# A vision tower's last mixture-of-experts layer: its outputs combined in groups of four tokens, shared by three engines

## The chip, the cores and the metric

The kernel runs on one core of a Trainium2 chip. The metric is the device time of one execution in microseconds. Three executions of the kernel before are given, with their median, and one more was recorded by the hardware profiler; all durations below are from that one.

## What is computed

The reference is a small vision tower in float32: patches of 128 images become 16 tokens each of 192 features, then follow a quantized attention, a mixture of 4 experts with one choice for each token, a linear attention, and a mixture of 8 experts with two choices. All of them add to the residual h. The change touches the last step alone, and in it only the last sum:

```python
h = h + _L1_ffn_ref(_layernorm(h, axis=-1), ...)
    # _L1_ffn_ref:
    top_p, top_i = jax.lax.top_k(router_probs, 2)
    top_p = top_p / jnp.sum(top_p, axis=-1, keepdims=True)
    ...                                     # the two chosen experts' outputs: o
    o = jnp.einsum('btck,btk->btc', o, top_p)   # p0 * out0 + p1 * out1
```

So each token's new value is h + p0 * (output of its first expert) + p1 * (output of its second).

## The kernel before, in words

Each engine has its own instruction stream, and they meet at semaphores. The residual h lies in SBUF as 128 partitions (images) x 16 tokens x 192 features.

Both mixture layers work alike. VectorE chooses the experts and works out where each token goes (route); SyncE writes the normalized rows to memory (rows_out, four stores of four tokens, lines 305 to 311); GpSimd gathers 128 rows at a time by an indirect DMA and scatters the results of each tile of 128 rows back by another (exchange, lines 403 to 424); TensorE multiplies, ScalarE applies Gelu (gelus), VectorE copies the results out of PSUM (copies). Layer 1 has 39 such tiles. The scattered results lie in DRAM in the tensor made, the first choices of all tokens ahead of the second choices.

When all scatters of the layer have landed, SyncE reads made back in outputs_in (line 326): for the first choice four loads of four tokens each, then four for the second, 384 KB each, into got[0] (the buffer xn) and got[1] (in the arena). Each load has a semaphore of its own. After layer 0 VectorE adds got[0] to h in four steps and goes on; there is only one choice there.

After layer 1 comes the end of the kernel. VectorE runs 32 scalar_tensor_tensor operations on line 1574, each h[:, t] = got[s][:, t] * pk[:, s, t] + h[:, t] for one token t of every image, over 192 elements in each partition: first all 16 tokens of the first choice, a link (the engine waits until its own last result is written), then all 16 of the second. pk holds the two weights of each token. A memset signals h_final, SyncE stores the whole of h in one transfer of 1536 KB (line 353) and waits for it. ScalarE has nothing to do after its last Gelu, and GpSimd nothing after its last scatter.

In the early weights stage (lines 380 to 398) GpSimd adds and multiplies weight tiles of 128 x 576 and other widths, and ScalarE scales others with a factor for each partition (line 446). Lines 1082 to 1101 are VectorE's statistics of the tokens, which run at the same time.

Of the kernel before, what the change touches and what calls it, by code (L numbers as in the profile page):

```python
# [10 lines left out]
ALU = mybir.AluOpType  # L11
ACT = mybir.ActivationFunctionType
# [6 lines left out]
NTOK = GRID * GRID  # L19
TOKS = IMGS * NTOK  # L20
# [30 lines left out]
C_P = 468  # L51
# [18 lines left out]
def build(nc, x_strips, x_blocks, tok_w, tok_w_un, tok_gb, tok_b, consts, qkv_w, qkv_b, proj_w, proj_b,  # L70
          gate0_w, gate0_b, ffn0_a, ffn0_b, ffn0_2, ffn0_b2, lin_q, lin_kT, lin_vT, lin_oT, lin_gT,
          gate1_w, ffn1_a, ffn1_b, ffn1_2, rows0, rows1, made0, made1, out):
    with ExitStack() as ctx:
# [186 lines left out]
        def _(sp):  # L260
# [65 lines left out]
            def outputs_in(F):  # L326

                n = F["n"]
                for u in range(4):
                    sp.wait_ge(sem(f"y_st{n}{u}"), 16 * ((F["tiles"] + 3 - u) // 4))  # L330
                for s in range(F["sel"]):
                    made = F["made"][TOKS * s:TOKS * s + TOKS, :].rearrange("(b t) c -> b t c", t=NTOK)
                    for i in range(4):
                        sp.dma_start(got[s][:, 4 * i:4 * i + 4, :], made[:, 4 * i:4 * i + 4, :]).then_inc(sem(f"back{n}_{4 * s + i}"), 16)

            sp.wait_ge(sem("wTr_ready"), 4)
            sp.dma_start(F0["w2"], ffn0_2).then_inc(sem("ffn_in0"), 16)
# [11 lines left out]
            rows_out(F1)  # L349
            up_weights(F1)  # L350
            outputs_in(F1)
            sp.wait_ge(sem("h_final"), 1)
            sp.dma_start(out, h[:]).then_inc(sem("out_done"), 16)
            sp.wait_ge(sem("out_done"), 16)


        @block.gpsimd
        def _(pool):
            steps = [0]

            def link(ins):

                steps[0] += 1
                ins.then_inc(sem("pool_step"), 1)
                pool.wait_ge(sem("pool_step"), steps[0])


            pool.memset(xT1[K1:128, :], 1.0).then_inc(sem("ones_row"), 1)
            pool.wait_ge(sem("ones_row"), 1)
            link(pool.memset(wnat[96:128, 5:7, :], 0.0))  # L370
            pool.memset(wnat[64:128, 4, :], 0.0).then_inc(sem("wnat_set"), 1)
            pool.wait_ge(sem("wnat_set"), 1)
            link(pool.memset(grid, 0.0))
            pool.memset(grid[:, :, :, 0:6:3], float(BFEAT // 2)).then_inc(sem("grid_set"), 1)
            pool.wait_ge(sem("grid_set"), 1)
            pool.wait_ge(sem("gb_in"), 16)
            for b in COLS:
                pool.wait_ge(sem(f"w_in{b}"), 48 if inner(b) else 32)
            pool.wait_ge(sem("wg_scaled"), len(TRIPLES))
            pool.wait_ge(sem("wg_added"), 4)  # L380
            for n, (P, b) in enumerate(TRIPLES):
                k = w_chunk(P, b)
                half = slice(3 * P, 3 * P + 3)
                beta = gb[:, 30 + k:33 + k].unsqueeze(2).to_broadcast([128, 3, DIM])
                link(pool.tensor_tensor((prod if n > 1 else sum_b)[:, half], w_sh[:, k:k + 3, :], beta, ALU.mult))
                if n > 1:
                    link(pool.tensor_tensor(sum_b[:, half], sum_b[:, half], prod[:, half], ALU.add))
                if n > 1:
                    link(pool.tensor_tensor(sum_g[:, half], sum_g[:, half], wg[:, k:k + 3, :], ALU.add))
                else:  # L390
                    link(pool.tensor_copy(sum_g[:, half], wg[:, k:k + 3, :]))
            beta = gb[:, 54:60].unsqueeze(2).to_broadcast([128, 6, DIM])
            link(pool.tensor_tensor(prod, w_un, beta, ALU.mult))
            link(pool.tensor_tensor(sum_b, sum_b, prod, ALU.add))
            for s in (sum_g, sum_b):
                link(pool.tensor_tensor(s[:, 0:3, :], s[:, 0:3, :], s[:, 3:6, :], ALU.add))
                link(pool.tensor_tensor(s[:, 0, :], s[:, 0, :], s[:, 1, :], ALU.add))
                pool.tensor_tensor(s[:, 0, :], s[:, 0, :], s[:, 2, :], ALU.add).then_inc(sem("w_sums"), 1)

            pool.wait_ge(sem("o_ps"), 4)  # L400
            pool.memset(aqT1[K1:K1 + 3], 1.0).then_inc(sem("ones_row"), 1)  # L401

            def exchange(F):

                n, N = F["n"], F["tiles"]

                def load(k):
                    pool.indirect_dma_start(sx[:, k % 4], None, F["src"],  # L408
                                            bass.IndirectOffsetOnAxis(from_i[:, k:k + 1], 0)).then_inc(sem(f"sx_in{n}{k % 4}"), 16)

                pool.wait_ge(sem(f"rows_out{n}"), 64)
                pool.wait_ge(sem(f"places{n}"), 1)
                for k in range(4):
                    load(k)
                pool.wait_ge(sem(f"x_ps{n}"), 1)
                load(4)

                for k in range(N):
                    pool.wait_ge(sem(f"y_out{n}"), k + 1)
                    pool.indirect_dma_start(F["made"], bass.IndirectOffsetOnAxis(to_i[:, k:k + 1], 0), yo[:, k % 4],  # L420
                                            None).then_inc(sem(f"y_st{n}{k % 4}"), 16)
                    if k + 5 < N:
                        pool.wait_ge(sem(f"x_ps{n}"), k + 2)
                        load(k + 5)

            exchange(F0)
            exchange(F1)


        @block.scalar  # L430
        def _(act):
# [202 lines left out]
            act.wait_ge(sem("soft_in"), 1)  # L634
            act.activation(rt[:, 128:256], rt[:, 128:256], ACT.Exp).then_inc(sem("soft_exp"), 1)
            gelus(F1)


        @block.tensor
        def _(pe):  # L640
# [205 lines left out]
            def router(F):  # L846
# [27 lines left out]
                pe.matmul(ps[:, 5, 0:cols], cst[:, C_TRI:C_TRI + 128], oh, start=True, stop=True)  # L874
                pe.matmul(ps[:, 6, 0:cols], ones, oh, start=True, stop=True).then_inc(sem("rank_ps"), 1)

                pe.wait_ge(sem(f"hot{n}"), 1)
                for c in range(16 * F["sel"]):
                    mm = pe.matmul(ps[:, 7, 0:2 * F["tiles"]], place[:, c, :], in_tile(F)[:, c].rearrange("p a k -> p (a k)"),
                                   start=(c == 0), stop=(c == 16 * F["sel"] - 1))  # L880
# [106 lines left out]
        def _(dve):  # L987
# [403 lines left out]
            def route(F):  # L1391
# [57 lines left out]
                for c in range(per):  # L1449
# [4 lines left out]
                                       tile.unsqueeze(2).to_broadcast(wide), ALU.is_equal))  # L1454
                link(dve.tensor_tensor(hot[:, :, 1, :], hot[:, :, 0, :],
                                       cst[:, C_TILE + 1:C_TILE + 1 + per].unsqueeze(2).to_broadcast(wide), ALU.mult))
                dve.tensor_scalar(hot[:, :, 0, :], hot[:, :, 0, :], cst[:, C_P:C_P + 1], None, ALU.mult).then_inc(sem(f"hot{n}"), 1)

                tk = rt[0:1, 1280:1280 + (E - 1) * N].rearrange("p (e k) -> p e k", e=E - 1)
                link(dve.tensor_tensor(tk, cst[0:1, C_TILE:C_TILE + N].unsqueeze(1).to_broadcast([1, E - 1, N]),  # L1460
# [20 lines left out]
                link(dve.scalar_tensor_tensor(none, row, 0.0, dump, ALU.is_lt, ALU.mult))  # L1481
                if n:
                    link(dve.scalar_tensor_tensor(row, second, float(TOKS), row, ALU.mult, ALU.add))
                dve.tensor_tensor(to_i[:, 0:N], row, none, ALU.add).then_inc(sem(f"places{n}"), 1)  # L1484

            def copies(F):
                n, N = F["n"], F["tiles"]
# [39 lines left out]
                dve.memset(w[K1:128], 0.0)  # L1527
            dve.tensor_copy(wgx1[0:K1], wgT1[0:K1].unsqueeze(2).to_broadcast([K1, 8, 16])).then_inc(sem("lin_set"), 1)
            for i in range(4):
                dve.wait_ge(sem(f"back0_{i}"), 16)  # L1530
                hs = h[:, 4 * i:4 * i + 4, :].rearrange("p a b -> p (a b)")
                link(dve.tensor_tensor(hs, hs, xnf[:, 768 * i:768 * i + 768], ALU.add))
                ins = ln_stats(4 * i, 4 * i + 4)
# [33 lines left out]
            transposed(3)  # L1567
            route(F1)
            copies(F1)
            for s in range(2):  # L1570
                for t in range(NTOK):
                    if t % 4 == 0:
                        dve.wait_ge(sem(f"back1_{4 * s + t // 4}"), 16)
                    ins = dve.scalar_tensor_tensor(h[:, t, :], got[s][:, t, :], pk[:, s, t:t + 1], h[:, t, :], ALU.mult, ALU.add)  # L1574
                link(ins)
            dve.memset(stat[:, 0:1], 0.0).then_inc(sem("h_final"), 1)


# [98 lines left out]
```

## Time and profile before

| | us |
|---|---|
| median of three executions | 692.64 |
| lowest, highest | 691.56, 694.15 |
| the profiled execution | 691.0 |
| its span, from first to last instruction | 689.2 |
| TensorE busy in it | 506.5 (73%) |
| VectorE busy in it | 354.6 (51%) |
| ScalarE busy in it | 163.7 (24%) |
| GpSimd busy in it | 156.5 (23%) |

The profiled execution's time is 1.8 us more than its span: that lies around the first and last instruction. The shares are means over stages with different limits. For a change at one place the chain of waits and the timeline are of more use, since they show which wait ends last there. Tiles carry the names of their buffers: xn and arena, where the combination is meant, are got[0] and got[1], and stat, rt and others are small work areas. GpSimd's durations are rougher than the other engines'.

### The profile page before, as it was taken

The page shows a single profiled execution, that of the slowest core. Times are in us where ns is not written, and L with a number is a line of the kernel's source. Part 1 is how long each engine was busy: PE and PEld are TensorE (multiplying, and loading weights), DVE is VectorE, ACT ScalarE, POOL GpSimd, SP SyncE. Part 2 cuts the span into 40 slices and gives each one's busy share as a digit, 9 for nine tenths or more (in the row PEclk, how much of TensorE's full clock was granted, in tenths as well). Part 3 has the DMA queues.
Part 4 walks back from the last instruction along what each step waited for, and adds up shares of the span by engine and source line. Part 5 has one row for each costly group of instructions (what it writes and reads, how often), then busy time and mean ns, then how long its engine had stood idle before and what let it go on. Part 6 is the DMA issues. An engine that isn't in the chain of part 4 may idle for free.

```text
span 689.2 us, 13111 instructions
## 1 busy us (share of the span) xinstructions
PE 506.5 (73%) x4632; PEld 450.1 (65%) x4633; DVE 354.6 (51%) x1088; ACT 163.7 (24%) x341; POOL 156.5 (23%) x156
## 2 busy tenths in 40 slices
PE   4999996996314516199999269621899999999960
PEld 4999996456313413189998266401799999999960
DVE  1599995466999885522212567667122212222216
ACT  4100001223793224043332040300221222112210
POOL 2894000000001000224442100001244444444320
PEclk9999998998656558599999789865799999999995
DMA  9960000000004002376659500202666555655516
GB/s 327 412 220 11 1 1 0 2 3 2 1 0 162 1 0 92 81 206 178 176 161 351 179 1 0 92 0 64 186 175 178 174 164 172 179 173 160 139 48 249
DMA packets 35235, 81.41 MB, mean 118 GB/s; under 512 B 6870, under 2 KB 17970, under 8 KB 34034
## 3 DMA queue, kind: packets, MB, share of 16 engines
q1 hardware_dynamic: 29618, 69.36, 30.8%
q0 software_dynamic: 5568, 11.41, 6.3%
q8 instruction: 29, 0.48, 0.3%
q14 instruction: 20, 0.16, 0.1%
HBM read 70.33 MB, written 10.42 MB: 117 GB/s over the span
## 4 chain that ended last, share of the span: by engine, by line
PE 63%; DVE 23%; DMA 5%; ACT 4%; issue 3%; SPq 1%; POOL 0%; ACTq 0%; DVEq 0%; POOLq 0%
PE ps L925 17%; PE ps L680 13%; PE ps L905 11%; PE ps L909 7%; DMA xT<-rows,from_i 2%; DVE stat L1028 2%; PE ps L750 2%; PE ps L751 2%; DVE h L1574 2%; PE ps L778 1%; PE ps L864 1%; DMA arena<-tok_w 1%; DVE xT L1450 1%; PE ps L890 1%; PE ps L655 1%
## 5 line engine op out<-in xcount | busy, mean ns | idle before, releaser
L925 PE MATMUL ps<-arena,xn 128*128 x696 | 128.1, 334 | 0.6 <-ACT xn L596 0.6
L925 PEld LDWEIGHTS ps<-arena,xn 128*128 128x128 f32 x696 | 111.5, 190 | 7.5 <-issue 0.8
L680 PE MATMUL ps<-arena 128*128 128x192 f32 (+1 forms) x672 | 99.1, 334 | 9.1 <-ACT arena L446 8.5
L680 PEld LDWEIGHTS ps<-arena 128*128 128x128 f32 (+1 forms) x672 | 97.4, 195 | 9.8 <-ACT arena L446 8.2
L408 POOL DMA_INDIRECT xT<-rows,from_i x58 | 56.5, 973 | 181.8 <-DVE to_i L1484 164.7
L420 POOL DMA_INDIRECT made<-xT,to_i x58 | 57.2, 987 | 155.5 <-DVE xT L1507 99.9
L905 PE MATMUL ps<-xT,arena 128*128 128x128 f32 x696 | 89.7, 280 | 0.0
L905 PEld LDWEIGHTS ps<-xT,arena 128*128 128x128 f32 x696 | 84.9, 197 | 0.1
L1507 DVE COPY xT<-ps 128x192 f32<-128x192 f32 x39 | 13.9, 357 | 134.1 <-PE ps L925 134.1
L599 ACT ACTIVATE xn<-ps 128x384 f32<-128x384 f32 x78 | 34.0, 488 | 137.2 <-PE ps L910 129.8
L909 PE MATMUL ps<-xT,arena 64*128 64x128 f32 x348 | 54.8, 292 | 0.0
L910 PE MATMUL ps<-xT,arena 64*128 64x128 f32 x348 | 54.8, 292 | 0.0
L909 PEld LDWEIGHTS ps<-xT,arena 64*128 64x128 f32 x348 | 43.6, 189 | 7.2 <-issue 0.5
L596 ACT ACTIVATE xn<-ps,b_all 128x128 f32<-128x128 f32 x114 | 31.4, 378 | 51.3 <-PE ps L910 51.3
L910 PEld LDWEIGHTS ps<-xT,arena 64*128 64x128 f32 x348 | 43.6, 189 | 0.0
L1505 DVE TENSOR_TENSOR xT<-ps,arena 128x192 f32<-128x192 f32 x19 | 6.8, 358 | 66.1 <-PE ps L925 66.1
L401 POOL MEMSET arena<- 3x2048 bf16 x1 | 1.8, 1797 | 156.0 <-PE ps L817 156.0
L644 PE MATMUL ps<-cst 128*128 128x128 f32 x54 | 10.7, 384 | 30.6 <-DVE stat L1037 30.6
L644 PEld LDWEIGHTS ps<-cst 128*128 128x128 f32 x54 | 9.7, 205 | 31.2 <-issue 15.7
L817 PE MATMUL ps<-arena 128*32 128x64 f32 x384 | 8.8, 268 | 28.0 <-DVE arena L1312 26.9
L890 PE MATMUL ps<-cst,xT 128*128 128x128 f32 x58 | 16.7, 288 | 16.2 <-DMA xT<-rows,from_i 15.2
L1492 DVE COPY xT<-ps 128x128 f32<-128x128 f32 x58 | 16.6, 286 | 22.5 <-PE ps L891 21.3
(339 smaller groups left out, 740.8 us busy)
## 6 DMA issues: line engine op xcount, KB each, us to landing
arena<-ffn_a SPq DMA_DIRECT2D x58, 384.0 KB
arena<-ffn_b SPq DMA_DIRECT2D x116, 96.0 KB
arena<-x_blocks SPq DMA_DIRECT2D x16, 384.0 KB, 7.2
arena<-x_strips SPq DMA_DIRECT2D x3, 1536.0 KB, 12.2
arena<-ffn SPq DMA_DIRECT2D x4, 1152.0 KB, 11.5
rows<-xn SPq DMA_DIRECT2D x8, 384.0 KB, 2.5
xn<-made SPq DMA_DIRECT2D x8, 384.0 KB, 4.2
arena<-tok_w SPq DMA_DIRECT2D x8, 288.0 KB, 7.4
```

The lines of the kernel that those rows point to most:

```text
L408: pool.indirect_dma_start(sx[:, k % 4], None, F["src"], bass.IndirectOffsetOnAxis(from_i[:, k:k + 1], 0)).then_inc(sem(f"sx_in{n}{k % 4}") ...
L420: pool.indirect_dma_start(F["made"], bass.IndirectOffsetOnAxis(to_i[:, k:k + 1], 0), yo[:, k % 4], None).then_inc(sem(f"y_st{n}{k % 4}"), 16)
L596: ins = act.activation(hT[:, u, 128 * c:128 * c + 128], ps[:, 1 + 2 * u + half, 128 * (c % 3):128 * (c % 3) + 128], ACT.Gelu, bias=b1_all[ ...
L599: ins = act.activation(hT[:, u, 384 * half:384 * half + 384], ps[:, 1 + 2 * u + half, 0:384], ACT.Gelu_apprx_tanh)
L644: pe.transpose(ps[:, 7, 0:128], ones, ident)
L680: mm = pe.matmul(tok_ps(t), xs[rows, strip % GRID, 2 * j + b, 128 * c:128 * c + 128], wg[rows, w_chunk(P, b) + c, :], start=bank not in op ...
L890: pe.transpose(ps[:, 0, 0:128], sx[:, u, 0:128], ident)
L905: pe.matmul(o(c), w[:, 128 * c:128 * c + 128], sT[:, u, 0:128], start=(c % 3 == 0), stop=False, skip_group_check=True)
L909: m0 = pe.matmul(o(c), w[0:64, cols], sT[0:64, u, 128:256], start=False, stop=True, skip_group_check=True)
L910: m1 = pe.matmul(o(3 + c), w[64:128, cols], sT[64:128, u, 128:256], start=False, stop=True, skip_group_check=True)
L925: mm = pe.matmul(ps[:, 6 + u, 0:DIM], hT[:, u, 128 * c:128 * c + 128], F["w2"][:, bass.ds(e2 + DIM * c, DIM)], start=(c == 0), stop=(c == ...
L1492: dve.tensor_copy(sT[:, u, 0:128], ps[:, 0, 0:128])
```

## The change

Four things change. (1) outputs_in issues the loads in another order: group by group of four tokens, and in each group the first choice, then the second. (2) The work on a group is split: VectorE does its first two tokens as before (two operations for each choice); for the other two ScalarE multiplies got by the weights in place, and GpSimd, once both choices are scaled, adds first got[0] and then got[1] to h, two tokens (384 elements in a partition) in one operation. (3) SyncE stores h in four transfers of 384 KB, each when VectorE and GpSimd are done with that group. (4) Some semaphores, one for each layer before, are one counter now.

```diff
--- before.py
+++ after.py
@@ -328,10 +328,10 @@
                 n = F["n"]
                 for u in range(4):
                     sp.wait_ge(sem(f"y_st{n}{u}"), 16 * ((F["tiles"] + 3 - u) // 4))
-                for s in range(F["sel"]):
-                    made = F["made"][TOKS * s:TOKS * s + TOKS, :].rearrange("(b t) c -> b t c", t=NTOK)
-                    for i in range(4):
-                        sp.dma_start(got[s][:, 4 * i:4 * i + 4, :], made[:, 4 * i:4 * i + 4, :]).then_inc(sem(f"back{n}_{4 * s + i}"), 16)
+                for i in range(4):
+                    for s in range(F["sel"]):
+                        made = F["made"][TOKS * s:TOKS * s + TOKS, :].rearrange("(b t) c -> b t c", t=NTOK)
+                        sp.dma_start(got[s][:, 4 * i:4 * i + 4, :], made[:, 4 * i:4 * i + 4, :]).then_inc(sem(f"back_{4 * s + i}"), 16)
 
             sp.wait_ge(sem("wTr_ready"), 4)
             sp.dma_start(F0["w2"], ffn0_2).then_inc(sem("ffn_in0"), 16)
@@ -349,9 +349,11 @@
             rows_out(F1)
             up_weights(F1)
             outputs_in(F1)
-            sp.wait_ge(sem("h_final"), 1)
-            sp.dma_start(out, h[:]).then_inc(sem("out_done"), 16)
-            sp.wait_ge(sem("out_done"), 16)
+            for i in range(4):
+                sp.wait_ge(sem("h_final"), i + 1)
+                sp.wait_ge(sem("h_pool"), i + 1)
+                sp.dma_start(out[:, 4 * i:4 * i + 4, :], h[:, 4 * i:4 * i + 4, :]).then_inc(sem("out_done"), 16)
+            sp.wait_ge(sem("out_done"), 64)
 
 
         @block.gpsimd
@@ -409,7 +411,7 @@
                                             bass.IndirectOffsetOnAxis(from_i[:, k:k + 1], 0)).then_inc(sem(f"sx_in{n}{k % 4}"), 16)
 
                 pool.wait_ge(sem(f"rows_out{n}"), 64)
-                pool.wait_ge(sem(f"places{n}"), 1)
+                pool.wait_ge(sem("places"), n + 1)
                 for k in range(4):
                     load(k)
                 pool.wait_ge(sem(f"x_ps{n}"), 1)
@@ -425,6 +427,11 @@
 
             exchange(F0)
             exchange(F1)
+            for i in range(4):
+                pool.wait_ge(sem("got_scaled"), i + 1)
+                two = slice(4 * i + 2, 4 * i + 4)
+                link(pool.tensor_tensor(h[:, two, :], h[:, two, :], got[0][:, two, :], ALU.add))
+                pool.tensor_tensor(h[:, two, :], h[:, two, :], got[1][:, two, :], ALU.add).then_inc(sem("h_pool"), 1)
 
 
         @block.scalar
@@ -634,6 +641,12 @@
             act.wait_ge(sem("soft_in"), 1)
             act.activation(rt[:, 128:256], rt[:, 128:256], ACT.Exp).then_inc(sem("soft_exp"), 1)
             gelus(F1)
+            for i in range(4):
+                for s in range(2):
+                    act.wait_ge(sem(f"back_{4 * s + i}"), 16 if s else 32)
+                    for t in (4 * i + 2, 4 * i + 3):
+                        ins = act.activation(got[s][:, t, :], got[s][:, t, :], ACT.Copy, scale=pk[:, s, t:t + 1])
+                ins.then_inc(sem("got_scaled"), 1)
 
 
         @block.tensor
@@ -874,7 +887,7 @@
                 pe.matmul(ps[:, 5, 0:cols], cst[:, C_TRI:C_TRI + 128], oh, start=True, stop=True)
                 pe.matmul(ps[:, 6, 0:cols], ones, oh, start=True, stop=True).then_inc(sem("rank_ps"), 1)
 
-                pe.wait_ge(sem(f"hot{n}"), 1)
+                pe.wait_ge(sem("hot"), n + 1)
                 for c in range(16 * F["sel"]):
                     mm = pe.matmul(ps[:, 7, 0:2 * F["tiles"]], place[:, c, :], in_tile(F)[:, c].rearrange("p a k -> p (a k)"),
                                    start=(c == 0), stop=(c == 16 * F["sel"] - 1))
@@ -1454,7 +1467,7 @@
                                        tile.unsqueeze(2).to_broadcast(wide), ALU.is_equal))
                 link(dve.tensor_tensor(hot[:, :, 1, :], hot[:, :, 0, :],
                                        cst[:, C_TILE + 1:C_TILE + 1 + per].unsqueeze(2).to_broadcast(wide), ALU.mult))
-                dve.tensor_scalar(hot[:, :, 0, :], hot[:, :, 0, :], cst[:, C_P:C_P + 1], None, ALU.mult).then_inc(sem(f"hot{n}"), 1)
+                dve.tensor_scalar(hot[:, :, 0, :], hot[:, :, 0, :], cst[:, C_P:C_P + 1], None, ALU.mult).then_inc(sem("hot"), 1)
 
                 tk = rt[0:1, 1280:1280 + (E - 1) * N].rearrange("p (e k) -> p e k", e=E - 1)
                 link(dve.tensor_tensor(tk, cst[0:1, C_TILE:C_TILE + N].unsqueeze(1).to_broadcast([1, E - 1, N]),
@@ -1481,7 +1494,7 @@
                 link(dve.scalar_tensor_tensor(none, row, 0.0, dump, ALU.is_lt, ALU.mult))
                 if n:
                     link(dve.scalar_tensor_tensor(row, second, float(TOKS), row, ALU.mult, ALU.add))
-                dve.tensor_tensor(to_i[:, 0:N], row, none, ALU.add).then_inc(sem(f"places{n}"), 1)
+                dve.tensor_tensor(to_i[:, 0:N], row, none, ALU.add).then_inc(sem("places"), 1)
 
             def copies(F):
                 n, N = F["n"], F["tiles"]
@@ -1527,7 +1540,7 @@
                 dve.memset(w[K1:128], 0.0)
             dve.tensor_copy(wgx1[0:K1], wgT1[0:K1].unsqueeze(2).to_broadcast([K1, 8, 16])).then_inc(sem("lin_set"), 1)
             for i in range(4):
-                dve.wait_ge(sem(f"back0_{i}"), 16)
+                dve.wait_ge(sem(f"back_{i}"), 16)
                 hs = h[:, 4 * i:4 * i + 4, :].rearrange("p a b -> p (a b)")
                 link(dve.tensor_tensor(hs, hs, xnf[:, 768 * i:768 * i + 768], ALU.add))
                 ins = ln_stats(4 * i, 4 * i + 4)
@@ -1567,13 +1580,14 @@
             transposed(3)
             route(F1)
             copies(F1)
-            for s in range(2):
-                for t in range(NTOK):
-                    if t % 4 == 0:
-                        dve.wait_ge(sem(f"back1_{4 * s + t // 4}"), 16)
-                    ins = dve.scalar_tensor_tensor(h[:, t, :], got[s][:, t, :], pk[:, s, t:t + 1], h[:, t, :], ALU.mult, ALU.add)
-                link(ins)
-            dve.memset(stat[:, 0:1], 0.0).then_inc(sem("h_final"), 1)
+            for i in range(4):
+                for s in range(2):
+                    dve.wait_ge(sem(f"back_{4 * s + i}"), 16 if s else 32)
+                    for t in (4 * i, 4 * i + 1):
+                        ins = dve.scalar_tensor_tensor(h[:, t, :], got[s][:, t, :], pk[:, s, t:t + 1], h[:, t, :], ALU.mult, ALU.add)
+                    if s == 0:
+                        link(ins)
+                ins.then_inc(sem("h_final"), 1)
 
 
 # ---- launch: one core; inputs and outputs as the reference has them ----
```

## Rows read from the trace of the kernel before

**Rows 1.** The page: the span, and the chain's shares by engine.

```profile
span 689.2 us, 13111 instructions
...
PE 63%; DVE 23%; DMA 5%; ACT 4%; issue 3%; SPq 1%; POOL 0%; ACTq 0%; DVEq 0%; POOLq 0%
```

**Rows 2.** Chain of waits, last stretch: start us, us, engine, tiles, line, count.

```profile
669.28 3.47 DMA xn<-made
...
672.78 4.82 DVE h L1574 x15
...
677.73 0.42 DVE h L1574
...
678.17 5.36 DVE h L1574 x16
```

**Rows 3.** Timeline of the end; and the one store's time to landing.

```profile
683.68 0.34 SPq L353 DMA_DIRECT2D out<-h  x1
...
DMA to landing us min/median/max: 5.1/5.1/5.1
```

**Rows 4.** SyncE's first and eighth load; to landing: loads 1, 2, 4, 6, 8.

```profile
669.28 0.34 SPq L334 DMA_DIRECT2D xn<-made  x1
...
672.61 0.43 SPq L334 DMA_DIRECT2D arena<-made  x1
...
DMA to landing us min/median/max: 3.5/3.5/3.5
...
DMA to landing us min/median/max: 4.1/4.1/4.1
...
DMA to landing us min/median/max: 6.0/6.0/6.0
...
DMA to landing us min/median/max: 6.9/6.9/6.9
...
DMA to landing us min/median/max: 7.8/7.8/7.8
```

**Rows 5.** ScalarE: timeline of two stretches, then two groups by form (us, mean ns).

```profile
6.27 2.18 ACT L446 ACTIVATE arena<-arena 128x192 f32<-128x192 f32 x6
...
402.04 3.62 ACT L581 ACTIVATE xn<-h,stat 128x192 f32<-128x192 f32 x8 [21.17 <-DVE stat L1043]
...
L446 ACT ACTIVATE arena<-arena 128x192 f32<-128x192 f32 x24 | 8.6, 441 | 4.4 <-DMA arena<-tok_w 4.4
...
L599 ACT ACT_TABLE_LOAD x1 | 1.3, 1283 | 37.6 <-PE ps L910 37.6
```

**Rows 6.** Groups by form of GpSimd, whole span: its tensor_tensor by width.

```profile
L396 POOL TENSOR_TENSOR arena<-arena 128x576 f32<-128x576 f32 x2 | 2.8, 1400 | 0.1
L394 POOL TENSOR_TENSOR arena<-arena 128x1152 f32<-128x1152 f32 x1 | 2.6, 2627 | 0.1
L393 POOL TENSOR_TENSOR arena<-arena 128x1152 f32<-128x1152 f32 x1 | 2.1, 2110 | 0.1
...
L397 POOL TENSOR_TENSOR arena<-arena 128x192 f32<-128x192 f32 x2 | 1.3, 631 | 0.2
```

**Rows 7.** Timeline where VectorE's operations meet GpSimd's adds.

```profile
53.49 1.40 POOL L396 TENSOR_TENSOR arena<-arena 128x576 f32<-128x576 f32 x1
...
53.85 1.10 DVE L1095 TENSOR_TENSOR stat<-stat 128x32 f32<-128x32 f32 x1
...
54.98 0.65 POOL L397 TENSOR_TENSOR arena<-arena 128x192 f32<-128x192 f32 x1
54.98 0.19 DVE L1096 SCALAR_TENSOR_TENSOR stat<-stat 128x32 f32<-128x32 f32 x1
...
55.21 0.45 DVE L1097 SCALAR_TENSOR_TENSOR stat<-stat 128x16 f32<-128x16 f32 x1
...
55.69 0.18 DVE L1098 TENSOR_TENSOR stat<-stat 128x16 f32<-128x16 f32 x1
```

**Rows 8.** The stores of rows_out: time to landing, all eight.

```profile
DMA to landing us min/median/max: 2.3/2.5/2.7
```

## The prediction, made before the changed kernel ran

> **What bounds the kernel now.** I read the page first for the size of things: TensorE is busy 73% of the span, and the chain that ended last lies 63% on it and 23% on VectorE [rows 1]. That is an average over the whole program. The change touches only what follows the last expert tile, so the place to read is the end of the chain of waits [rows 2]. There TensorE has no part. Once the last scatter has landed, SyncE sends the eight loads from 669.28 on, VectorE waits until 669.28 + 3.47 = 672.75 for the first, then runs 32 scalar_tensor_tensor (16 + 16) without a hole worth naming up to 683.53, and one store is issued at 683.68. The span ends at 689.2, so the last stretch is 5.5 us of a store that nothing covers [rows 1 to 3]. So the last 20 us are: loads 3.5, VectorE 10.8, store 5.5.
>
> When does each load land? The eight are issued at 669.28, 669.67, 670.14, 670.62, 671.09, 671.66, 672.14 and 672.61 (the first and the last stand in [rows 4]); the times to landing of the first, second, fourth, sixth and eighth are 3.5, 4.1, 6.0, 6.9 and 7.8 us [rows 4]. So they are in at 672.8, 673.8, 676.6, 678.6 and 680.4; the third, fifth and seventh at 674.7, 677.6 and 679.5. The reader should see two things. The last load is in 3.1 us before VectorE is done, so VectorE and not memory sets the end of the combination. And the loads are spaced by about 1 us each (a gap of 1.9 once), so pairs of loads arrive every 1.9 to 2.8 us.
>
> **Part 1, the order of the loads.** The same eight transfers of the same size are sent; only which bytes come first changes. I take the landing times as unchanged and read them as pairs: both choices of group 0 are there at 673.8, of group 1 at 676.6, of group 2 at 678.6, of group 3 at 680.4. Cost nothing; what it gives is that tokens can be finished, and stored, before all is loaded. For the first expert layer the order is the same as before.
>
> **Part 2, VectorE's half.** It keeps 16 of 32 operations. Alone they go at a pitch of 5.36 / 16 = 0.335 us [rows 2], so a group of four takes 1.34 us, less than the time between pairs. Alone, VectorE would end 0.7 us after the last load, at about 681.2, instead of 683.6: 2.4 us less. The link between the two choices costs about 0.1 us of pipeline drain per group (before, the step from the 16th operation at 677.73 to the next at 678.17 is 0.44 instead of 0.335 [rows 2]) and is hidden in the waits for loads, except in the last group.
>
> **Part 3, ScalarE's scaling.** Sixteen activations, 128x192 from SBUF to SBUF, Copy with a scale per partition. The early weights stage holds the identical form: six in 2.18 us, so a pitch of 0.35 us, mean of one 0.44 [rows 5]. ScalarE has had nothing to do since its last Gelu. A table load would be 1.28 us, but the trace has table loads only at the start and on the lines of Ln, Exp and the two Gelus, and the eight Identity activations at 402.04, the first after the last Gelu of layer 0, start without one [rows 5], so I take none; if there were one it would fall in the wait for the first load. Per group, both choices scaled: the first choice's pair during the wait, the second's ends 0.35 + 0.44 = 0.8 us after its load. GpSimd is released at 674.7, 677.5, 679.4 and 681.3.
>
> **Part 4, GpSimd's adds.** Eight tensor_tensor of 128x384, in place, both inputs in SBUF. The trace has none of this width, but the same form at 192 and 576 [rows 6]: 0.63 and 1.40 us. Linear between them, 384 is 1.01. Bounds: 0.81, if it profits like the multiply with a broadcast input (2.11 at 1152, where the add takes 2.63), and 1.26 (two of 192). I take 1.01, since 1152 of the same form at 2.63 lies on nearly the same line, and 0.08 from one to the next, as between 53.49 + 1.40 and 54.98 in [rows 7]. (Durations of GpSimd are rough in such traces; here each start follows the end before it, so the pitch bears them out.) A group is then 2.2 us. Alone GpSimd would run 674.7 to 676.9, 677.5 to 679.7, to 681.8, to 684.0. So even without any contention GpSimd, not VectorE, now ends last, and no earlier than VectorE ended before (683.6). What the split takes from VectorE it gives back on GpSimd.
>
> **Part 5, both at once.** This is the term that decides. In the weights stage VectorE meets GpSimd in the trace of before [rows 7]. A tensor_tensor of 128x32 on VectorE that starts at 53.85, while GpSimd's add runs from 53.49 to 54.89, takes 1.10 us and ends at 54.95; the next operation of the same shape takes 0.19. Likewise one of 128x16 takes 0.45 beside the 0.65 us add, against 0.18 for the same shape next. Both end 0.03 to 0.06 us after GpSimd's. VectorE's operation waits for GpSimd's to end. The other way round is fainter: the add that starts together with the 0.19 us operation takes 0.65, where the mean of its line is 0.63 and so the other one 0.61; so VectorE's short operation holds GpSimd for about 0.04 us, about what its 32 elements need. The blocked operations have two inputs. The new scalar_tensor_tensor reads h and got, two inputs in SBUF, and GpSimd's adds read h and got too, so I take it that they exclude one another.
>
> From the first GpSimd add at 674.7, the shared path has to pass 8 adds x 1.01 = 8.1 us and VectorE's remaining 12 operations (four are done before). If an operation of VectorE holds it for its whole pitch these are 12 x 0.335 = 4.0 us; if only for its data (0.04 us at 32 elements, so 0.2 to 0.24 at 192) 2.4 to 2.9. Ends: 674.7 + 8.1 + 2.4 = 685.2 and 674.7 + 8.1 + 4.0 = 686.8, with 0 to 0.5 us of holes while both wait for group 1. Following the operations one after another, first come first served, with 0.2, I get GpSimd done at 684.7 and VectorE, which is let in one operation at a time, last at 686.2; with 0.335, 685.6 and 687.1. I take 686.2, since the rows are nearer to the short hold.
>
> The Trainium skill says the same against this change (SBUF — State Buffer, "Who interferes with whom"): a VectorE instruction with two inputs in SBUF and a GpSimd instruction that reads SBUF exclude each other, and whichever issues first keeps the pair for its whole instruction. The first half is what the trace shows (1.10 against 0.19 us); the second half is not what the add of 0.65 against 0.61 us shows. By the page VectorE's 12 would count in full, and the sum would end at 687.1.
>
> **Part 6, the stores.** One store of 1536 KB, 5.1 us from issue to landing, becomes four of 384 KB. The same size and the same way out of SBUF stands in rows_out: 2.3 to 2.7, median 2.5 us [rows 8]. The first three are issued at about 677, 680 and 683 and are covered. Only the last counts. All loads were issued by 673.1, so the stores queue behind them on SP's ring and don't hold them up; if they shared bandwidth with the last loads it would cost up to 1 us (384 KB at the rate of one load per us). SyncE waits in turn for both halves of a group; nothing else is queued behind it.
>
> **Part 7, the shared semaphores.** hot, places and back are counted on instead of being separate: same waits, no time.
>
> **The sum.** Before: compute ends 683.6, store 683.68 + 5.1 = 688.8, then 0.4 to the end of the span, 689.2. After: 686.2 + 0.1 to the issue + 2.5 + 0.4 = 689.2. The store gives 2.6 us, the later end of the combination takes 2.6. Difference 0; bounds of the two holds and the holes 688.2 to 690.3, so -1.0 to +1.1 (an add of 0.81 or 1.26 instead of 1.01 would move it by another -1.6 or +2.0, and I give little to either). The profiled execution took 691.0 (1.8 outside the span); the median of the three runs is 692.64, 1.6 above it. I add the difference to the median: 692.6.
>
> **Rivals.**
> - No exclusion that matters (the adds and VectorE's operations interleave at full speed, or VectorE slips wholly into the 0.08 us gaps). GpSimd ends at 684.0; 684.1 + 2.5 + 0.4 = 687.0, a gain of 2.2: 690.4. For it: VectorE's operations are short, and the early rows touched tiny ones only. Against: both rows that meet an add wait to its end.
> - Slower: hand-over between the two engines. If each change of owner costs idle time, there are some 12 blocked operations of VectorE and up to 8 adds; the rows show 0.03 to 0.06 us for a change, which is inside my bounds. A price of 0.17 us over 20 changes would be 3.5 us and pass 0.5%; the add itself reaching 1.45 us instead of 1.01 would do the same. Then 696.1 or more. Break-even against before is right where I stand: every 0.1 us on an add is 0.8 us slower.
> - Stores and last loads disturb each other: + 1.0, 693.6.
> - Faster by over 0.5%: that needs the last add by 682.7. But the last load is in at 680.4, scaled at 681.2, and two adds are 2.1: 683.3 at the earliest, 686.3 at the end of the span, a gain of 2.9 us or 0.42%. Only a shift elsewhere in the program would lift it over.
>
> **How the numbers follow.** Forecast 0.55, at 692.6. No exclusion 0.2. Disturbed stores 0.1. Hand-over or slow adds 0.09. Over 0.5% faster, with help from elsewhere, 0.06. A measurement of this kernel can tell about 0.5%, 3.5 us, from no change; its own runs lie between 691.56 and 694.15. The range goes from 690.0 (no exclusion, less a little for the spread of the runs) to 694.8 (bound of the forecast, 693.7, plus about 1). Faster 0.07, same 0.84, slower 0.09.
>
> **What would show it.** In the after trace: GpSimd's adds near 1.0 us, the last of them ending between 684 and 686; VectorE's scalar_tensor_tensor from group 1 on no longer at 0.42 us or less each but some at over 1 us, ending just after an add; ScalarE done by 681.3; stores at about 677, 680 to 683, and a last one near 686.2 landing 2.5 us later. If the adds overlap VectorE's operations with both at their own durations, Part 5 is wrong and the result is 690.4. If the loads land later than 680.4, Part 1 is. If an add is well over 1.2 us, Part 4 is.

## The result, and the profile after

Over 20 executions of each kernel, measured side by side, the changed kernel took 694.15 us (692.40 to 697.98) and the kernel before 691.76 (689.88 to 695.85): a ratio of 1.0040, 95% interval 1.0024 to 1.0056. So it is slower by 0.4%, about 2.8 us by the ratio (the two medians lie 2.4 us apart). The profiled execution took 693.63 us, its span was 691.8.

First the part that the prediction worked out, the combination. The timeline of the changed kernel from the last scatter on (start us, us, engine, line, operation; answers to [rows 2, 3]):

```profile
667.14 0.97 POOL L422 DMA_INDIRECT made<-xT,to_i  x1 [0.98 <-DVE xT L1520]
...
669.61 0.34 SPq L334 DMA_DIRECT2D xn<-made  x1
...
674.78 0.99 POOL L433 TENSOR_TENSOR h<-h,xn 128x384 f32<-128x384 f32 x1 [6.67 <-ACT arena L648]
...
675.00 2.06 DVE L1587 SCALAR_TENSOR_TENSOR h<-xn,pk,h 128x192 f32<-128x192 f32 x2 [0.28 <-DMA xn<-made]
675.85 0.99 POOL L434 TENSOR_TENSOR h<-h,arena 128x384 f32<-128x384 f32 x1
676.91 8.65 SPq L355 DMA_DIRECT2D out<-h  x4
...
680.90 0.80 ACT L648 ACTIVATE arena<-arena,pk 128x192 f32<-128x192 f32 x2
...
682.03 1.11 POOL L433 TENSOR_TENSOR h<-h,xn 128x384 f32<-128x384 f32 x1
682.21 2.21 DVE L1587 SCALAR_TENSOR_TENSOR h<-xn,pk,h 128x192 f32<-128x192 f32 x2
683.22 0.99 POOL L434 TENSOR_TENSOR h<-h,arena 128x384 f32<-128x384 f32 x1
684.46 0.75 DVE L1587 SCALAR_TENSOR_TENSOR h<-arena,pk,h 128x192 f32<-128x192 f32 x2
```

GpSimd's first add starts at 674.78 and its last ends at 684.21; VectorE ends at 685.2. Beside the adds two operations of VectorE take 2.06 to 2.21 us together, alone 0.75. The last store is issued at 685.23 and takes 2.3 us to land. That is 687.6, and yet the span ends at 691.8. The instructions at the very end of each engine's stream, which the kernel's end puts there, show why (engine, operation, duration in ns min/median/max, first and last start):

```profile
L73 POOLq DRAIN  x1: 8387/8387/8387, 683.2 to 683.2; - x1
L73 SPq COMPARE_BRANCH  x1: 41/41/41, 687.6 to 687.6; - x1
L73 SPq DRAIN  x1: 7/7/7, 687.7 to 687.7; - x1
L73 SPq EVENT_SEMAPHORE  x1: 17/17/17, 691.7 to 691.7; - x1
```

and so do the waits of SyncE's queue (waited for: us in total, times, longest):

```profile
SPq L73 <- PEq L73: 4.0, 1, 4.0
SPq L73 <- DMA out<-h: 2.0, 1, 2.0
```

At the end of the program each engine has a drain, an instruction that ends only after the engine's last one has, and then meets the others. SyncE is ready at 687.7. GpSimd's drain begins with its last add, at 683.2, and ends at 691.6, 7.4 us after that add ended. All others wait for it for 4.0 us. (The row of waits names TensorE's queue; that drain was over long before, and GpSimd's is the one that ends there.) The same instruction stood in the trace of the kernel before, among rows that were not read for the prediction:

```profile
L73 POOLq DRAIN  x1: 8548/8548/8548, 666.6 to 666.6; - x1
...
L73 SPq DRAIN  x1: 7/7/7, 688.9 to 688.9; - x1
```

There it ran from 666.6 to 675.1, under the loads and VectorE's work, and cost nothing.

To compare traces I use one measure, from the start of the last scatter on GpSimd to the end of the span. It leaves out the 666 to 672 us of work ahead of it, which vary by some us between executions. Before: 689.2 - 666.8 = 22.4. Changed: 691.8 - 667.1 = 24.7. The difference of 2.3 us agrees with the 2.8 (1.7 to 3.9) that the ratio gives. Each value of this measure below is from one profiled execution; where the same kernel was profiled twice, it came to 21.0 and 21.1 us, and a single load can land 0.3 to 0.5 us earlier or later.

### The profile page after: what moved, and what is told of

It reads as the page before. It is cut to its first block, busy times and chain, and to the rows that moved or that the text cites. A ratio compares the mean times of both kernels' runs of the same rounds, so it can differ in the third digit from the quotient of the medians.

```text
span 691.8 us, 13128 instructions
## 1 busy us (share of the span) xinstructions
PE 507.6 (73%) x4632; PEld 451.1 (65%) x4633; DVE 354.9 (51%) x1071; ACT 170.2 (25%) x357; POOL 164.4 (24%) x164
## 4 chain that ended last, share of the span: by engine, by line
PE 63%; DVE 22%; DMA 6%; ACT 4%; issue 3%; SPq 1%; POOL 0%; DVEq 0%; ACTq 0%; POOLq 0%
PE ps L938 17%; PE ps L693 13%; PE ps L918 11%; PE ps L922 7%; DMA xT<-rows,from_i 3%; DVE stat L1041 2%; PE ps L763 2%; PE ps L764 2%; DMA xn<-made 1%; PE ps L791 1%; PE ps L668 1%; PE ps L877 1%; DMA arena<-tok_w 1%; DVE xT L1463 1%; PE ps L670 1%
## 5 line engine op out<-in xcount | busy, mean ns | idle before, releaser
L922 PE MATMUL ps<-xT,arena 64*128 64x128 f32 x348 | 54.1, 289 | 0.0
L923 PE MATMUL ps<-xT,arena 64*128 64x128 f32 x348 | 54.1, 289 | 0.0
L903 PE MATMUL ps<-cst,xT 128*128 128x128 f32 x58 | 16.7, 288 | 16.9 <-DMA xT<-rows,from_i 16.9
L1505 DVE COPY xT<-ps 128x128 f32<-128x128 f32 x58 | 16.6, 286 | 22.5 <-PE ps L904 21.3
```

Of the source, the lines that this page charges most:

```text
L903: pe.transpose(ps[:, 0, 0:128], sx[:, u, 0:128], ident)
L922: m0 = pe.matmul(o(c), w[0:64, cols], sT[0:64, u, 128:256], start=False, stop=True, skip_group_check=True)
L923: m1 = pe.matmul(o(3 + c), w[64:128, cols], sT[64:128, u, 128:256], start=False, stop=True, skip_group_check=True)
L1505: dve.tensor_copy(sT[:, u, 0:128], ps[:, 0, 0:128])
```

## The experiments

Three theories stand behind the expectations. Theory 1: the drain of GpSimd, which now starts with its last add instead of its last scatter, sets the end. Theory 2: the drain is only how the profile draws a wait, and the loss is elsewhere. Theory 3: the loss is the exclusion of VectorE and GpSimd.

**The drain by itself, on the kernel before.** One tiny memset is the only addition:

```diff
             exchange(F1)
+            pool.wait_ge(sem("h_final"), 1)
+            pool.memset(stat[:, 1:2], 0.0)
```

> The kernel before, with one memset of one element per partition added on GpSimd, which waits until VectorE has ended the combination (683.7 in the trace of before). Nothing else changes; the store is issued at the same time. Theory 1 (GpSimd's drain after its last instruction takes about 7.4 us from the end of that instruction, and the end of the kernel waits for it): the drain starts at 683.8 and ends at 691.2 to 691.4, 2.2 us after the span of before (689.2); the time rises by 2 to 2.5 us, ratio about 1.003. Theory 2 (the end is set by the combination and the stores, and the drain of 8 us seen in the trace is only the profile's way of drawing a wait for the other engines): 0 us, ratio 1.000, and the drain shrinks to what is left until the store lands.

Measured: ratio 1.0024 (0.9993 to 1.0055), 24.3 us from the last scatter (669.7) to the end (694.0). The rows of its trace:

```profile
686.28 0.34 SPq L353 DMA_DIRECT2D out<-h  x1
686.32 0.10 POOL L429 MEMSET stat<- 128x1 f32 x1 [15.64 <-DVE stat L1578]
...
L73 POOLq DRAIN  x1: 7460/7460/7460, 686.3 to 686.3; - x1
L73 SPq DRAIN  x1: 7/7/7, 691.6 to 691.6; - x1
```

A memset of 0.1 us, 16.6 us after the start of the last scatter, moves the end of the span by 1.9 us (24.3 - 22.4). SyncE is ready at 691.6, GpSimd at 693.8. The drain's time is real: the end waits for it, and it runs after GpSimd's last instruction although GpSimd had been idle for 15.6 us. Theory 2 expected the drain to shrink to the store's landing, and it did not. The time alone, with 1 inside its interval, would not have settled this; the rows do.

**An early drain in the changed kernel.**

```diff
             exchange(F1)
+            pool.drain()
             for i in range(4):
                 pool.wait_ge(sem("got_scaled"), i + 1)
```

> The changed kernel, with one drain instruction added on GpSimd after its last scatter, while it has nothing to do until 674.8. It tells what the 8 us are. If they are the clearing up of the indirect DMAs, done once: the early drain takes about 8.5 us (667 to 675.5), the drain at the end is short, the last store landing (about 687.6 in the changed kernel's trace) sets the end, and the span is about 688 to 689 instead of 691.8. If every drain of GpSimd costs it: two of about 8 us, the first delays the adds by about 1 us, and the span is 692 to 693. If a drain is cheap while it waits for nothing: the early one is short and the last one 8 us, span 691.8.

Measured: 21.0 us from the last scatter to the end (671.9 to 692.9). Its two drains, the early one on line 430 and the one at the end:

```profile
L430 POOLq DRAIN  x1: 8547/8547/8547, 671.7 to 671.7; - x1
...
L73 POOLq DRAIN  x1: 1092/1092/1092, 687.8 to 687.8; - x1
L73 SPq DRAIN  x1: 7/7/7, 692.6 to 692.6; - x1
```

So the 8.5 us are owed once. Spent early, under the loads, they leave 1.1 us for the end, which is just the last add, and the last store ends the kernel again. It is not quite free: it ends at 680.3, and the first add, for which ScalarE was done at 679.5, starts only then. The same kernel again, now timed:

> The changed kernel with a drain of GpSimd after its last scatter, now timed. In the one look its last drain was 1.1 us and the stretch from the last scatter to the end 21.0 us, against 22.4 before and 24.7 changed. Theory 1: 1.4 us less than before and 3.7 less than the changed kernel, ratio to before 0.998. If the look was luck and drains don't matter: ratio 1.004 as for the changed kernel.

Measured: ratio 0.9987 (0.9971 to 1.0004), 21.1 us from the last scatter (667.56) to the end (688.7). One line turns the changed kernel from 0.4% slower into one that can't be told from the kernel before; its interval lies clear of the changed kernel's. In its trace SyncE's side ends last again, and the span ends at 688.7:

```profile
L73 POOLq DRAIN  x1: 1094/1094/1094, 683.6 to 683.6; - x1
L73 SPq DRAIN  x1: 7/7/7, 688.5 to 688.5; - x1
```

**GpSimd's adds without VectorE's half.** This kernel leaves out VectorE's 16 operations, so half of the tokens lack the last sum.

```diff
-                    for t in (4 * i, 4 * i + 1):
-                        ins = dve.scalar_tensor_tensor(h[:, t, :], got[s][:, t, :], ...)
...
+                dve.memset(stat[:, i:i + 1], 0.0).then_inc(sem("h_final"), 1)
```

> The changed kernel without VectorE's 16 operations (so the first two tokens of each group are stored without the last layer's sum; the output lacks that part); a memset of one element stands in for them. It takes away all that could exclude GpSimd's adds. Times are read from the start of the last scatter to the end of the span: 22.4 us before, 24.7 changed. Theory 1 (GpSimd's drain, 7.4 us after its last add, sets the end; VectorE's operations delay it by little): adds of 0.99 us at a pitch of 1.07 instead of some of 1.11, GpSimd done 0.2 to 0.6 us earlier, the stretch 24.1 to 24.5 us. Theory 3 (the loss is the exclusion of the two engines): the stretch falls to that of before or below, 22.4 or less.

Measured: 24.1 us (671.8 to 695.9). All eight adds take 0.99 us. The drain began with the last add and ended at 695.7, while SyncE was ready at 690.9:

```profile
L73 POOLq DRAIN  x1: 8387/8387/8387, 687.3 to 687.3; - x1
L73 SPq DRAIN  x1: 7/7/7, 690.9 to 690.9; - x1
```

So the exclusion, though plain in the rows, is not what lengthened the kernel: without it 0.6 of the 24.7 us go, the lower end of what theory 1 allowed. Even of these 0.6 about 0.3 are no exclusion: the fourth load was in 9.5 us after the last scatter's start here and 9.8 us in the changed kernel. Theory 3 falls.

**GpSimd done one group earlier.** The last group's two adds go to VectorE, GpSimd's loop runs over three groups:

```diff
+                if i < 3:
+                    sp.wait_ge(sem("h_pool"), i + 1)
...
-            for i in range(4):
+            for i in range(3):
                 pool.wait_ge(sem("got_scaled"), i + 1)
...
+                if i == 3:
+                    dve.wait_ge(sem("got_scaled"), 4)
+                    link(dve.tensor_tensor(h[:, 14:16, :], h[:, 14:16, :], got[0][:, 14:16, :], ALU.add))
+                    ins = dve.tensor_tensor(h[:, 14:16, :], h[:, 14:16, :], got[1][:, 14:16, :], ALU.add)
```

> The changed kernel with the last group's two adds on VectorE instead of GpSimd. GpSimd's last add is that of group 2, which in the changed kernel ended 2.15 us before that of group 3. Theory 1: the end of the span moves earlier by the same 2.1 us, from 24.7 to 22.5 us after the last scatter's start, although VectorE now has more to do (4 operations and 2 adds after the last load, its last store issued at about the old time or 0.5 us earlier). Theory 3 (exclusion and late stores set the end): the end follows VectorE's last operation, and moves by less than 0.7 us.

Measured: 22.5 us (666.8 to 689.3). The rows of its end:

```profile
680.73 0.99 POOL L435 TENSOR_TENSOR h<-h,arena 128x384 f32<-128x384 f32 x1
...
L73 POOLq DRAIN  x1: 8388/8388/8388, 680.7 to 680.7; - x1
L73 SPq DRAIN  x1: 7/7/7, 687.0 to 687.0; - x1
```

The end follows GpSimd's last add, with the same 7.4 us behind it, and not SyncE, which is ready 2.1 us earlier.

**What the drain depends on.** The run with the late memset, with a drain between the two expert layers as well (the last two lines stood there already):

```diff
             exchange(F0)
+            pool.drain()
             exchange(F1)
             pool.wait_ge(sem("h_final"), 1)
             pool.memset(stat[:, 1:2], 0.0)
```

> The kernel before with the late memset on GpSimd (as in the run where its drain of 7.46 us ended the kernel), and a drain after the first expert layer's 19 tiles, long before the last 39. It asks what the time of a drain depends on. If on the number of indirect DMAs since the last drain (38 + 78 = 116 for 7.4 us, so 0.064 us each): the first drain is 2.4 us, the last 5.0 us, and the stretch from the last scatter to the end of the span falls from 24.3 to 22.3 or so (then the store ends it). If it is one fixed price after any indirect DMA: 7.4 us both times and 24.3.

```profile
L427 POOLq DRAIN  x1: 4382/4382/4382, 384.3 to 384.3; - x1
...
L73 POOLq DRAIN  x1: 6549/6549/6549, 683.8 to 683.8; - x1
```

Measured: 23.3 us, between the two forecasts. The drain's time grows with what GpSimd did since the one before, but not as a plain share of the indirect DMAs. Counted from the end of GpSimd's last instruction: 38 DMAs, 3.2 us, 0.083 each; 78 DMAs, 6.4 us, 0.082 each. All 116 at such a rate would be some 9.6, and 7.4 is seen. A price for each with a cap near 90 would fit the three numbers; three numbers don't prove it. What GpSimd does in this time no row shows, and no run is without indirect DMAs, so that they are what the drain pays for is likely (eight adds after the early drain left nothing behind) but not shown. Both stay open.

**The parts of the change without GpSimd.** First the four stores alone, on the kernel before:

```diff
+                    if s == 1 and t % 4 == 3:
+                        ins.then_inc(sem("h_final"), 1)
...
+            for i in range(4):
+                sp.wait_ge(sem("h_final"), i + 1)
+                sp.dma_start(out[:, 4 * i:4 * i + 4, :], h[:, 4 * i:4 * i + 4, :]).then_inc(sem("out_done"), 16)
```

> The kernel before with one part of the change alone: VectorE does all 32 operations in the old order and the loads come in the old order, but each group of four tokens is stored when its second choice is added (the extra memset at the end goes). Both theories: VectorE ends at 683.5 as before, the last store of 384 KB lands 2.3 to 2.5 us after its issue instead of 5.1, so the span ends at 686.3 to 686.6, 2.6 us less than before, ratio 0.996. If the four stores hinder each other, the last one lands later than 2.5 us after its issue.

Measured: ratio 0.9962 (0.9937 to 0.9987), 19.7 us (672.4 to 692.1), 2.7 less than before. Each store landed 2.3 to 2.4 us after its issue, so they don't hinder each other:

```profile
683.96 5.36 DVE L1575 SCALAR_TENSOR_TENSOR h<-arena,pk,h 128x192 f32<-128x192 f32 x16
685.40 4.28 SPq L354 DMA_DIRECT2D out<-h  x4
...
DMA to landing us min/median/max: 2.3/2.3/2.4
```

Then order, stores and ScalarE's scaling as changed, but VectorE adds:

```diff
-                sp.wait_ge(sem("h_pool"), i + 1)
...
-            for i in range(4):
-                pool.wait_ge(sem("got_scaled"), i + 1)
-                two = slice(4 * i + 2, 4 * i + 4)
-                link(pool.tensor_tensor(h[:, two, :], h[:, two, :], got[0][:, two, :], ALU.add))
-                pool.tensor_tensor(h[:, two, :], h[:, two, :], got[1][:, two, :], ALU.add).then_inc(sem("h_pool"), 1)
...
-                ins.then_inc(sem("h_final"), 1)
+                dve.wait_ge(sem("got_scaled"), i + 1)
+                two = slice(4 * i + 2, 4 * i + 4)
+                link(dve.tensor_tensor(h[:, two, :], h[:, two, :], got[0][:, two, :], ALU.add))
+                dve.tensor_tensor(h[:, two, :], h[:, two, :], got[1][:, two, :], ALU.add).then_inc(sem("h_final"), 1)
```

> The changed kernel without GpSimd's adds: ScalarE scales as in the changed kernel, and VectorE does the two adds of 384 elements of each group itself (an add of 768 elements takes 0.94 us in the trace of before, so 0.55 each), besides its four operations. Order of loads and four stores stay. GpSimd is done at 667 and its drain by 676, so under theory 1 it is off the path. VectorE per group 4 x 0.335 + 2 x 0.5 + 0.2 of links = 2.5 us: 672.8 + 4 x 2.5 = 682.9 to 683.5 with the waits for loads. Last store 2.3 us, end of span 686.0 to 686.6: 2.6 to 3.2 us less than before, ratio 0.996, and 5 to 6 us less than the changed kernel. Theory 2 (what was lost is elsewhere than at the end of GpSimd's stream): at most the 0.5 to 1 us that the combination ends earlier.

Measured: ratio 0.9961 (0.9937 to 0.9984), 19.6 us (666.4 to 686.0). In its trace VectorE's pairs of operations take 0.75 us at every group and its adds 0.56, half of GpSimd's 0.99:

```profile
681.40 0.75 DVE L1581 SCALAR_TENSOR_TENSOR h<-arena,pk,h 128x192 f32<-128x192 f32 x2
682.07 0.55 DVE L1586 TENSOR_TENSOR h<-h,xn 128x384 f32<-128x384 f32 x1
682.65 0.56 DVE L1587 TENSOR_TENSOR h<-h,arena 128x384 f32<-128x384 f32 x1
```

Two comparisons with this run say what the parts are worth. The four stores alone came to 19.7 us, so the new order of the loads and ScalarE's scaling add only 0.1 us to what the stores give. And the changed kernel with the early drain came to 21.1, so even with its drain out of the way GpSimd is a worse place for the eight adds than VectorE, by 1.5 us.

VectorE is still the last, 3.1 us after the last load (672.14 + 8.0 = 680.1). So more of it went to ScalarE, three tokens of four, on top of the run before (GpSimd has no part here either):

```diff
-                    for t in (4 * i + 2, 4 * i + 3):
+                    for t in (4 * i + 1, 4 * i + 2, 4 * i + 3):
                         ins = act.activation(got[s][:, t, :], got[s][:, t, :], ACT.Copy, scale=pk[:, s, t:t + 1])
-                ins.then_inc(sem("got_scaled"), 1)
+                    ins.then_inc(sem("got_scaled"), 1)
...
+                    t, three = 4 * i, slice(4 * i + 1, 4 * i + 4)
+                    dve.scalar_tensor_tensor(h[:, t, :], got[s][:, t, :], pk[:, s, t:t + 1], h[:, t, :], ...)
+                    dve.wait_ge(sem("got_scaled"), 2 * i + s + 1)
+                    ins = dve.tensor_tensor(h[:, three, :], h[:, three, :], got[s][:, three, :], ALU.add)
```

> The version in which ScalarE scales and VectorE adds, now with three tokens of each group on ScalarE instead of two, each choice signalled by itself, and VectorE left with one scalar_tensor_tensor and one add of 576 elements for each choice; GpSimd has no part, four stores. VectorE per group 2 x 0.335 + 2 x 0.76 + 0.1 = 2.3 us instead of 2.6; ScalarE 6 x 0.36 = 2.2. Theory 1: what is left after the last load (3.1 us to VectorE's end in the two-token version) falls to about 2.1 to 2.4, so the stretch from the last scatter to the end is 18.6 to 19.2 us instead of 19.6, ratio to before 0.995. If ScalarE becomes the late one (each add waits 1.2 us for its scaling and VectorE can't work ahead), 19.5 to 20.5.

Measured: 688.74 us against 692.50, ratio 0.9944 (0.9918 to 0.9970), 19.1 us (666.05 to 685.2). Of all the versions it has the lowest ratio, 0.56% less than the kernel before. Against the two-token version the intervals overlap, so that it is the faster of the two is not shown by the times; the rows have it 0.4 us shorter, the lower end of what was expected. What is left after the last load fell as expected, from 3.1 to 2.2 us, but that load landed 0.5 us later here.

## Why the prediction was wrong

**The step that failed is the last term of the sum**, "0.4 to the end of the span". It took for granted that the last store ends the kernel after the change because it did so before. In the changed kernel the wait for GpSimd's drain ends last: 4.2 us from the store's landing at 687.6 to the end at 691.8 instead of 0.4. The terms account for the whole miss of 2.3 us: this one was 3.8 too small, the way to VectorE's end 1.3 too long (mostly part 5), and the last store with its issue 0.2 too long (part 6).

**No rival held it.** The slower rival was a hand-over price between the engines. The changed kernel's trace shows none: adds of 0.99 and 1.11 us at a pitch of 0.95 to 1.19, 1.07 in the mean of the last six. GpSimd was treated as ending with its last instruction. What should have been asked of each engine that gets new work at the end is what stands behind its last instruction now and how much cover it has: in the trace of before, a drain of 8.5 us with 14 us of cover. The new adds moved it 16.6 us later.

**That 694.15 us lies inside the range of 690.0 to 694.8 is luck.** The range was made for other reasons (the holds, the spread of the runs). The missing 3.8 us alone are more than the 2.2 us by which it goes above the forecast; the overpriced terms of parts 5 and 6 took 1.5 of them back. The prediction also held that nothing under 0.5% could be told from no change; the interval of the ratio came out at 0.16% to each side, enough to tell 0.4%.

**Part 1, loads: right.** In the changed kernel the first, second, fourth, sixth and eighth land 3.2, 3.9, 6.0, 7.1 and 8.0 us after their issues [rows 4: 3.5, 4.1, 6.0, 6.9, 7.8]. The first store, issued at 676.9 while four loads were still on their way, took 4.9 us, and that was covered. The last load took 0.2 us longer than before; whether the store is the reason is not shown.

**Parts 2 and 3: right.** VectorE's operations alone go in pairs of 0.75 us, ScalarE's in pairs of 0.80, with no table load, and ScalarE is done at 681.7, 0.8 us after the last load.

**Part 4, the adds: right.** 0.99 us where 1.01 was interpolated [rows 6].

**Part 5, exclusion: right in kind, too dear.** VectorE's operation waits for the end of an add as in [rows 7], one slipping in between adds. Five of VectorE's operations on the first choice that met an add (times in ns, min/median/max, then first and last start):

```profile
L1587 DVE SCALAR_TENSOR_TENSOR h<-xn,pk,h x5: 1108/1146/1149, 675.9 to 683.3; 128x192 f32<-128x192 f32 x5
```

1.15 us against 0.41 alone. The other way round the price was far lower than the 12 x 0.2 = 2.4 us of the sum: only two of the eight adds grew, from 0.99 to 1.11 us. Measured from the first load's issue, GpSimd ended after 14.6 us (684.2 - 669.6), forecast 15.4, and VectorE after 15.6 (685.2 - 669.6), forecast 16.9. The Trainium skill (SBUF — State Buffer, "Who interferes with whom") is borne out in that the two exclude each other with two inputs in SBUF on VectorE's side; that the pair is kept for VectorE's whole instruction is not: 0.12 us of delay against an instruction of 0.41.

The prediction also took two inputs for what the blocked operations have in common. In the trace of before, just after [rows 7], one with a single input waits as well; the same line much later, with GpSimd idle, is shown last:

```profile
56.28 1.40 POOL L396 TENSOR_TENSOR arena<-arena 128x576 f32<-128x576 f32 x1
56.38 1.33 DVE L998 TENSOR_SCALAR stat<-stat 128x16 uint32<-128x16 uint32 x1
...
435.61 0.18 DVE L998 TENSOR_SCALAR stat<-stat 128x16 uint32<-128x16 uint32 x1
```

So two inputs are not the condition in this kernel. For the forecast it makes no difference, since the operations of the change have two.

**Part 6, stores: right.** 2.3 us from issue to landing for the last, 2.5 forecast. The four stores alone gave the 2.6 us that the sum had for them (2.7 measured).

So without the drain the sum would have been too high rather than too low: it forecast no difference, and with the early drain the stretch is 21.1 us, 1.3 less than before.

## What to carry to other kernels

Before work is given to an engine that was done early, look at the end of its own stream: what is owed behind the last instruction there moves with it. In a kernel whose GpSimd issued indirect DMAs, let it drain while something else covers it, or leave it out of the tail. And where an exclusive pair of engines shares work, count it nearly as one engine, and give the work to the one that does it faster: an add of 384 elements took 0.56 us on VectorE and 0.99 on GpSimd. Here the smaller stores alone were worth 0.4%, loads in pairs and ScalarE's scaling nothing that the times can tell beyond that, and GpSimd's part took more than all of it back: 5.1 us (24.7 - 19.6), of which 3.6 went with the early drain.

## What the runs showed of the hardware

- In this kernel, with 116 indirect DMAs (58 gathers and 58 scatters), GpSimd's drain ends 7.3 to 7.4 us after its last instruction, even when it had been idle for 15.6 us before that; it is owed once, and after an early drain the next took 1.1 us, the last add itself. With 78 DMAs since the drain before it was 6.4 us, with 38 3.2.
- The drains of the other engines have no such tail. In the trace of the changed kernel that of ScalarE is 0.83 us, of VectorE 0.78 and of TensorE 2.38 long, but each begins while its engine's last instructions still run and ends within 0.1 us of their end.
- A scalar_tensor_tensor of VectorE of 192 elements that meets an add of GpSimd takes up to 1.15 us instead of 0.41; two of eight adds beside them took 1.11 instead of 0.99. A tensor_scalar with one input took 1.33 us beside an add and 0.18 alone.
